# A conditioned feed-forward block in f32: out projection as seven quarter products, condition product on TensorE, means by adding DMAs, centring on GpSimd

## The reference, cut to what matters

```python
xr = x.reshape(Bx, Tx, 8, LATENT)                                # 8 groups of 128
h = jax.nn.gelu(jnp.einsum('btel,elf->btef', xr, W1) + b1, approximate=False)   # 128 -> 512
y = (jnp.einsum('btef,efl->btel', h, W2) + b2).reshape(Bx, Tx, Dx)              # 512 -> 128
eo = jax.nn.silu(emb) @ emb_W + emb_b                            # (4,1024) @ (1024,2048)
scale, shift = jnp.split(eo[:, None, :], 2, axis=-1)
hn = _layernorm(y, ln_g, ln_b) * (1.0 + scale) + shift
return x + jax.nn.silu(hn) @ out_W + out_b                       # 1024 -> 1024
```

## Time and profile before

| | |
|---|---|
| runs | 706.33, 706.30, 706.07 us; median 706.3 |
| span of the profiled execution | 704.2 us, 8302 instructions |
| busy | PE 700.5 us (99%), DVE 603.7 (86%), ACT 469.3 (67%), POOL 104.1 (15%) |
| granted PE clock, mean | 0.999 |
| DMA | 133.22 MB, mean 189 GB/s |

### The profile page before, as it was taken

How to read it: one execution, slowest core, us unless ns; L and a number is a source line. 1 busy time by engine, 2 the same in 40 slices (tenths; PEclk the granted TensorE clock), 3 DMA queues, 4 the chain that set the end, 5 groups by cost and what they waited for, 6 DMA issues and landing times.

```text
span 704.2 us, 8302 instructions
## 1 busy us (share of the span) xinstructions
PE 700.5 (99%) x3082; PEld 577.9 (82%) x3082; DVE 603.7 (86%) x725; ACT 469.3 (67%) x526; POOL 104.1 (15%) x68
## 2 busy tenths in 40 slices
PE   9999999999999999999999999999999999999998
PEld 6888888888888888888888888888888888888887
DVE  6888999999999989899887999999999978677512
ACT  7898888888878879888883456454656454555500
POOL 0000000000000011100121332423232432322100
PEclk9999999999999999999999999999999999999999
DMA  6766557344232531332789687887699877565531
GB/s 240 247 232 207 187 203 231 109 169 150 90 121 90 209 120 61 120 107 104 210 293 301 183 279 233 275 256 246 219 293 264 256 217 210 183 176 143 156 120 60
DMA packets 51880, 133.22 MB, mean 189 GB/s; under 512 B 4096, under 2 KB 25216, under 8 KB 49408
## 3 DMA queue, kind: packets, MB, share of 16 engines
q1 hardware_dynamic: 46944, 115.79, 46.9%
q0 software_dynamic: 4608, 16.78, 12.3%
q10 hardware_dynamic: 288, 0.13, 0.1%
HBM read 82.35 MB, written 33.55 MB: 165 GB/s over the span
## 4 chain that ended last, share of the span: by engine, by line
PE 99%; DMA 0%; ACT 0%; DVE 0%; issue 0%; DVEq 0%
PE psum L949 48%; PE psum L939 25%; PE psum L923 25%; PE psum L1001 2%; DMA wraw<-in_W 0%; PE psum L971 0%; ACT W L534 0%; DVE res L901 0%; DVEq L125 0%
## 5 line engine op out<-in xcount | busy, mean ns | idle before, releaser
L665 DVE TENSOR_TENSOR g_lo<-g_raw,g_hi 128x1024 fp32r<-128x1024 f32 x128 | 158.4, 1239 | 27.9 <-ACT g_hi L495 25.3
L489 ACT ACTIVATE g_raw<-psum,cols 128x1024 f32<-128x1024 f32 x128 | 142.9, 1116 | 34.1 <-PE psum L923 24.9
L949 PE MATMUL psum<-oW_hi,s_lo 128*128 128x512 f32 x496 | 152.7, 389 | 0.0
L949 PE MATMUL psum<-oW_hi,s_hi 128*128 128x512 f32 x496 | 152.7, 389 | 0.0
L949 PE MATMUL psum<-oW_lo,s_hi 128*128 128x512 f32 x496 | 152.6, 389 | 0.0
L939 PE MATMUL psum<-g_hi,W 128*128 128x512 f32 x512 | 136.8, 389 | 0.0
L923 PE MATMUL psum<-xT_hi,W 128*128 128x512 f32 x508 | 135.8, 389 | 0.0
L939 PEld LDWEIGHTS psum<-g_hi,W 128*128 128x128 f32 x512 | 96.1, 188 | 20.0
L923 PEld LDWEIGHTS psum<-xT_hi,W 128*128 128x128 f32 x508 | 95.3, 188 | 19.8
L949 PEld LDWEIGHTS psum<-oW_hi,s_hi 128*128 128x128 f32 x496 | 93.1, 188 | 19.4
L949 PEld LDWEIGHTS psum<-oW_hi,s_lo 128*128 128x128 f32 x496 | 93.1, 188 | 19.3
(11 more groups left out here) (77 smaller groups left out, 679.8 us busy)
## 6 DMA issues: line engine op xcount, KB each, us to landing
y_scratch<-y_stage SPq DMA_DIRECT2D x32, 512.0 KB, 3.1
yb<-y_scratch SPq DMA_DIRECT2D x16, 1024.0 KB, 4.8
res<-in_x SPq DMA_DIRECT2D x32, 512.0 KB, 6.1
res<-out_b_all POOLq DMA_DIRECT2D x32, 512.0 KB, 4.5
xT_raw<-in_xT SPq DMA_DIRECT2D x31, 512.0 KB, 4.3
out<-res SPq DMA_DIRECT2D x31, 512.0 KB, 4.1
tail_cols<-in_emb_T SPq DMA_DIRECT2D x24, 512.0 KB, 7.2
wraw<-in_out_W SPq DMA_DIRECT2D x16, 256.0 KB, 4.9
```

The lines of the kernel that those rows point to most:

```text
L489: nc.scalar.activation(g_raw[:, m % 2], ring(m), ACT.Gelu, bias=cols[:, R_B1 + k:R_B1 + k + 1]).then_inc(gelu_done, 1)
L665: nc.vector.tensor_tensor(g_lo[:, m % 2], g_raw[:, m % 2], g_hi[:, m % 2].bitcast(F32), ALU.subtract).then_inc(glo_done, 1)
L949: mm = nc.tensor.matmul(proj(q)[:, half], v[:, g, cut], w[:, g, half], start=(g == 0 and k == 0), stop=(g == G - 1 and k == 2))
```

## The change

The out projection of a pair is the product of a 2 x 2 block matrix A (token tiles 2p, 2p + 1 by feature halves 0 to 511, 512 to 1023) with out_W in quarters B11, B12, B21, B22. It is now computed in seven products of half-size blocks (the Strassen-Winograd form) instead of eight. DVE forms four sums of blocks of A (`sums12`, `sum3`, `sum4`), POOL four of out_W (T1 to T4, in stage 1). Each product is 12 matmuls of 512 columns (4 groups, 3 parts). The products P1, P2, P6, P5, P7, P3, P4 are made in this order; three go on accumulating into one PSUM bank `z`, two into `y5`, and DVE adds each bank to `res` after each product (`add`, seven times 512 columns per pair, instead of twice 1024). The weights of B22, T3 and T4 are written to DRAM in stage 1 (`wc_scratch`, split into hi and lo) and read back at the end of it, into places that stage 1 leaves.

The condition's product is 32 f32 matmuls on PE (`condition`), between chunks 24 and 25, from emb_W in SBUF (8 MB, loaded at items 1 to 4); DVE copies the result out, it goes through DRAM to be transposed (ACT's DMA at item 9), and there are no dots. The sums over groups for the mean are made by DMAs from POOL's queue that accumulate each `y_stage` tile into `y_sum` in DRAM (`add_y`); stage_y(n) waits until the one of n - 2 has landed. From pair 3 on POOL centres (`centre`, two of 128 x 1024 f32) and scales the mean, DVE does so for pairs 0 to 2. DVE's norm reads the reciprocal from PSUM, as before; one half of the squares goes to PSUM from pair 3 on.

```diff
...
+    y_sum = nc.dram_tensor("y_sum", [NP, P, TP], F32, kind="Internal").ap()
+    emb_rows = nc.dram_tensor("emb_rows", [B, NE * P], F32, kind="Internal").ap()
+    wc_scratch = nc.dram_tensor("wc_scratch", [3, 2, P, HG, BANK], F32, kind="Internal").ap()
...
+                    load_wc(C_T3, LO, t3)
+                    for q in range(2, 4):
+                        load_res(q)
...
             sp.wait_ge(glo_done, M)
+            load_wc(C_T3, HI, t3)
+            sp.wait_ge(s2_done, M)
+            load_wc(C_B22, HI, b22)
+            load_wc(C_B22, LO, b22)
+            load_wc(C_T4, LO, t4)
+            sp.wait_ge(y_staged, N)
+            g, t = ORDER[N - 1]
+            sp.dma_start(y_scratch[PT * t:PT * t + PT, :, g].rearrange("h p t -> p h t"),
+                         y_stage[:, (N - 1) % 2].rearrange("p (h t) -> p h t", h=PT)).then_inc(y_stored[(N - 1) % 2], 16)
+            sp.wait_ge(s_sum, 4)
+            sp.wait_ge(dlo_done, 1)
+            sp.wait_ge(alo_done, 1)
+            load_y(3)
             for s in range(2):
                 sp.wait_ge(y_stored[s], 16 * (N // 2))
+            for t in range(NT):
+                sp.wait_ge(y_summed[t], 16 * G)
+            load_wc(C_T4, HI, t4)
...
+            def add_y(n):
+                t = ORDER[n][1]
+                k = sums_before(n) - 1
+                pool.wait_ge(y_staged, n + 1)
+                place = y_sum[PT * t:PT * t + PT].rearrange("h p t -> p h t")
+                part = y_stage[:, n % 2].rearrange("p (h t) -> p h t", h=PT)
+                if k == 0:
+                    pool.dma_start(place, part).then_inc(y_summed[t], 16)
+                else:
+                    pool.wait_ge(y_summed[t], 16 * k)
+                    pool.dma_start(place, part, accum_op=ALU.add).then_inc(y_summed[t], 16)
...
+            def centre(p, h):
+                pool.wait_ge(y_landed[p % 3], 16 * (p // 3 + 1))
+                pool.wait_ge(mean_scaled, p - 2)
+                part = yb[p % 3][:, half_of(h)]
+                nc.gpsimd.tensor_tensor(part, part, mean_all[:].unsqueeze(1).to_broadcast([P, HG, TP]), ALU.subtract
+                                        ).then_inc(centred, 1)
+            def scale_mean(p):
+                pool.wait_ge(mean_done, p + 1)
+                nc.gpsimd.tensor_scalar(mean_all[:], mean_all[:], 1.0 / D, None, ALU.mult).then_inc(mean_scaled, 1)
+            for n in range(N):
+                ...
+                add_y(n)
             pool.wait_ge(out_b_landed, 16)
             for q in range(2):
                 add_bias(q)
+            for p in range(NP):
+                if p + 2 < NP:
+                    var_of(p + 2)
+                if 1 <= p and p + 3 < NP:
+                    mean_of(p + 3)
+                if p + 3 < NP:
+                    scale_mean(p + 3)
+                    centre(p + 3, 0)
+                    centre(p + 3, 1)
+                if p + 1 < NP:
+                    add_bias(2 * p + 2)
+                    add_bias(2 * p + 3)
...
+                if (n, c) == (VISIT + 3, 3):
+                    act.wait_ge(rows_stored, 4 * 16)
+                    act.dma_start(emb_dots[:], emb_rows.rearrange("b (q p) -> p b q", p=P), allow_slow_non_contiguous=True).then_inc(dots_landed, 16)
...
+            act.wait_ge(mod_step, 6)
+            silu(1, 0)
             stage_y(N - 1)
+            round_d(0, 2)
+            for p in range(NP):
                 if p + 1 < NP:
+                    silu(p + 1, 1)
+                    round_d0(p + 1)
+                    round_a22(p + 1)
+                if p + 2 < NP:
+                    nc.scalar.preload_act_table(ACT.Sqrt)
+                    root(p + 2, std_ps)
                     nc.scalar.preload_act_table(ACT.Silu)
+                if p + 1 < NP:
+                    round_d(p + 1, 1)
+                if p + 3 < NP:
+                    square(p + 3, 0)
+                    square(p + 3, 1)
+                if p + 2 < NP:
+                    silu(p + 2, 0)
+                if p + 1 < NP:
+                    round_d(p + 1, 2)
...
+            left, right = slice(0, BANK), slice(BANK, D)
+            for p in range(NP):
+                if p >= 1:
+                    add(p - 1, P4, z_ps(p - 1), 1, left)
+                rest_d(p, 2)
+                if p + 2 < NP:
+                    var_sum_first(p + 2)
+                add(p, P1, z_ps(p), 0, left)
+                if p + 2 < NP:
+                    var_sum_rest(p + 2)
+                if p + 1 < NP:
+                    rest_d0(p + 1)
+                add(p, P2, y2_ps, 0, left, of=P1)
+                if p + 1 < NP:
+                    sums12(p + 1)
+                    rest_a22(p + 1)
+                add(p, P6, z_ps(p), 0, right)
+                add(p, P5, y5_ps, 1, right)
+                if p + 2 < NP:
+                    invert(p + 2, rstd_ps, std_ps)
+                if p + 1 < NP:
+                    sum3(p + 1)
+                add(p, P7, z_ps(p), 1, right, of=P5)
+                if p + 2 < NP:
+                    norm(p + 2, 0, rstd_ps)
+                if p + 1 < NP:
+                    sum4(p + 1)
+                add(p, P3, y5_ps, 0, right, of=P6)
+                if p + 2 < NP:
+                    norm(p + 2, 1, rstd_ps)
+                if p + 1 < NP:
+                    rest_d(p + 1, 1)
...
+            def condition():
+                pe.wait_ge(cond_step, 2)
+                pe.wait_ge(emb_landed, 16 * KC)
+                pe.wait_ge(y_staged, VISIT)
+                for k in range(KC):
+                    for j in range(4):
+                        mm = nc.tensor.matmul(psum[32 * j:32 * j + B, VISIT_BANK], cond_s[:, k],
+                                              emb_raw[:, k, j * BANK:(j + 1) * BANK], start=(k == 0), stop=(k == KC - 1))
+                mm.then_inc(cond_done, 1)
+            def product(to, hi, lo, w_hi, w_lo, low_ready, begin=True, passes=range(3), cut=slice(0, BANK)):
+                for k in passes:
+                    v, w = ((hi, w_hi), (hi, w_lo), (lo, w_hi))[k]
+                    if k == 2:
+                        pe.wait_ge(*low_ready)
+                    for g in range(HG):
+                        mm = nc.tensor.matmul(to[:, cut], v[:, g], w[:, g, cut], start=(begin and k == 0 and g == 0),
+                                              stop=(k == 2 and g == HG - 1), skip_group_check=not begin)
+                if 2 in passes:
+                    mm.then_inc(prod_done, 1)
...
+                    begin_pair0(range(2))
+                if m == C * VISIT:
+                    condition()
...
+            for p in range(NP):
+                hi = [d_hi[(3 * p + i) % 4] for i in range(3)]
+                lo = [d_lo[(3 * p + i) % 4] for i in range(3)]
+                z = z_ps(p)
+                f, s = slice(0, HG), slice(HG, G)
+                if p == 0:
+                    begin_pair0(range(2, 3))
+                    pe.wait_ge(gelu_done, M)
+                else:
+                    if p >= 2:
+                        pe.wait_ge(added, 7 * (p - 2) + P4)
+                    pe.wait_ge(dhi_done, 3 * p + 1)
+                    product(z, hi[0][:, f], lo[0][:, f], wa[:, A_B11, HI], wa[:, A_B11, LO], (dlo_done, 3 * p + 1))
+                    pe.wait_ge(added, 7 * (p - 1) + P2)
+                product(y2_ps, hi[0][:, s], lo[0][:, s], wa[:, A_B21, HI], wa[:, A_B21, LO], (dlo_done, 3 * p + 1))
+                pe.wait_ge(dhi_done, 3 * p + 2)
+                pe.wait_ge(added, 7 * p + P1)
+                product(z, hi[1][:, f], lo[1][:, f], wa[:, A_T2, HI], wa[:, A_T2, LO], (dlo_done, 3 * p + 2), begin=False)
+                if p >= 1:
+                    pe.wait_ge(added, 7 * (p - 1) + P3)
+                product(y5_ps, hi[1][:, s], lo[1][:, s], wa[:, A_T1, HI], wa[:, A_T1, LO], (dlo_done, 3 * p + 2))
+                pe.wait_ge(dhi_done, 3 * p + 3)
+                pe.wait_ge(added, 7 * p + P6)
+                if p == 0:
+                    pe.wait_ge(wc_landed[C_T3], 32)
+                product(z, hi[2][:, f], lo[2][:, f], t3[HI], t3[LO], (dlo_done, 3 * p + 3), begin=False)
+                pe.wait_ge(added, 7 * p + P5)
+                if p == 0:
+                    pe.wait_ge(wc_landed[C_B22], 32)
+                product(y5_ps, hi[2][:, s], lo[2][:, s], b22[HI], b22[LO], (dlo_done, 3 * p + 3), begin=False)
+                pe.wait_ge(ahi_done, p + 1)
+                pe.wait_ge(added, 7 * p + P7)
+                if p == 0:
+                    pe.wait_ge(wc_landed[C_T4], 32)
+                if p < NP - 1:
+                    product(z, a_hi[p % 2], a_lo[p % 2], t4[HI], t4[LO], (alo_done, p + 1), begin=False)
+            for k in range(2):
+                product(last_ps[k], a_hi[p % 2], a_lo[p % 2], t4[HI], t4[LO], (alo_done, NP),
+                        cut=slice(k * TP, (k + 1) * TP))
```

(37 more changed lines are left out.)

871 lines of the change are left out of this document (415 added, 456 removed).

## The result

The changed kernel takes **838.1 us** (median of 4 runs, 836.2 to 840.0) against 706.3 (706.1 to 706.9): ratio 1.186, 95% interval 1.183 to 1.189. The forecast was 696, the range 678 to 717. It was wrong in sign, by 142 us.

A forecast was written before the change was run, and what follows sets the result against it. TensorE was taken to bound the kernel, 99% of the chain. 704.2 - 43.5 (seven products) + 8 (condition) + 0.5 (first stage) + 9.8 (VectorE against GpSimd) + 15 (change of stages) = 694.0; with 2.1, 696 us, range 678 to 717.

The forecast's parts named there:

- Seven products: Second stage, TensorE: a pair needs 84 matmuls instead of 96, 192 fewer over sixteen pairs; 43.5 us off.
- Condition: First stage, TensorE: 32 f32 products between two chunks, four sharing the array at once; 8 us on.
- Rival 1: Condition on TensorE: the f32 products don't overlap, 27.3 us instead of 8, total 715; chance 0.27.
- The loop through GpSimd: Second stage: one pair's round through GpSimd, ScalarE and VectorE takes 17.1 to 19.2 us with centrings of 2.3; just fits.
- VectorE against GpSimd: Second stage: overlap adds 0.9 us per reduction and 0.9 for both centrings; VectorE 19.7 a pair, 9.8 on over 14 pairs.
- Next to them stand mostly PSUM readers: Second stage: VectorE work beside GpSimd's centrings mostly reads PSUM, so both centrings together cost it only 0.9 us.
- Rival 2: Second stage: GpSimd holds VectorE through whole centrings, period 21.6 us, total 723; chance 0.13.
- First stage otherwise: First stage: VectorE and ScalarE stay ahead, GpSimd's y_sum transfers land in time; 0.5 us on, 0 to 10 allowed.
- Change of stages: Between stages: late second-stage weights, T4's high part last, stop TensorE in pair 0; 15 us on, range 5 to 20.
- The early bias wait lies inside the same wait: Change of stages: the late first bias, add P1 at 8 us or later instead of 4, adds nothing beyond the weight wait.
- The range: Whole kernel: forecast range 678 to 717 us, taking in rival 1 and half of rival 3, leaving out rival 2.

The follow-up runs named there:

- e9: e8 with the variance of pairs 3 to 15 as fp32r products on TensorE instead of VectorE's tree and GpSimd's reduction; 740.0 us, 739.9 when timed again.
- e1: The changed kernel with the second stage's centring back on VectorE, scaling folded in; GpSimd keeps reductions and bias transfers; 746.6 us.
- e4: The changed kernel with one GpSimd multiplication of 8 columns put between the two reductions, in 12 pairs; 995.8 us.
- e2: The changed kernel with a pair's two reductions as f32 products on TensorE, scaling gone, centring still on GpSimd; 762.4 us.
- e3: The changed kernel without the 32 adding transfers into y_sum and the waits on them, so its means are not the reference's; 810.4 us.
- e11: e1 with the adding transfers into y_sum made plain writes, so y_sum holds one group's y; 728.4 us.
- e10: e3 without GpSimd's 16 subtractions of out_W's quarters, so its output weights are not the reference's; 804.2 us.
- e5: e1 with the first two bias transfers issued ahead of the last adding transfer into y_sum; 755.0 us.
- e8: e1 with y_sum laid out in one 4 KB row per partition and item instead of shorter rows; 743.4 us.

## Why the prediction was wrong

- *Seven products, 43.5 off.* Right as a count of TensorE's work: matmuls are still 0.2267 us apart where nothing stops them, and e9's pairs come at 20.04 instead of 21.95. In the changed kernel none of it shows, as TensorE does not set the period.
- *Condition, 8 on.* Right: 7.05. Rival 1 is false.
- *The loop through GpSimd.* **This step failed, and is most of the 102 us of the second stage; with the centring taken off GpSimd (e1) 95 of them come back.** The loop had "two reductions 3.3 to 5.4, scaling 0.4, two centrings 2x, handovers 0.5". The centring was nearly right (2.4 to 3.4, mean 2.85, against 2.3 with 7.2 as the bound), the scaling was 0.9, and the part through ScalarE and VectorE, 8.3 by the rows, took 8.0 us or more. What had no term is GpSimd's change of code: 7.2 us from the reductions to the scaling, in full in each round, and 0.8 on average on the way back, where most of it hides beside the other engines' part. Together that is 8 of the 9 to 11 us between the forecast loop, 17.1 to 19.2, and the measured 27.8. The trace of before could not show it: there GpSimd ran no elementwise work in the second stage. I bounded the new operation's duration from both sides and never asked what stands between it and its neighbours. e4 puts the price at 6.6 us for each change added, and e1 and e2 take the changes away from either side.
- *VectorE against GpSimd, 0.9 for the two centrings.* Also wrong, and hidden behind the first error: 4.3 us a pair once the code no longer changes (e2). "Next to them stand mostly PSUM readers" failed; beside each centring an instruction with two SBUF inputs is caught and held until the centring has ended. Rival 2, with chance 0.13, named this, and put the period at 21.6; e2 has 21.92. That the two are near is luck: the 21.6 has 1.8 for reductions that e2 does not run, and 2.8 where e2 has 4.3. With the centring on VectorE the reductions cost about 1.1, less than the 1.8 I took, and the period is 20.38.
- *First stage otherwise, 0.5 on.* **Wrong: 37.6 on.** The step was "each transfer has two items, 21.8 us, before stage_y needs it, against 4.5 us to land for the accumulating ones now". The 4.5 is of an accumulation into SBUF, 4 KB rows; into DRAM it takes 8.8, and that still fits into two items: stage_y waits 0.2 us in all. What failed is that I priced only this wait. The transfers also keep x loads from landing (5.5 us instead of 4.3), and ScalarE, which takes x, gelu, out_W and y in one order, stands on a landing in front of 17 of its roundings of x. By the runs: sums in y_sum 18 (e3), of which the adding is 13 at this place (e11); GpSimd's subtractions 7.6 (e10, not clear of the spread); 12 remain, which I did not take apart. Candidates are the out_W roundings on ScalarE and VectorE, and loads of out_W that land in 12 us.
- *Change of stages, 15 on, T4's high part last.* The size was near (20.6), the place wrong: T4 is never waited for in the changed kernel, the first bias is. "The early bias wait lies inside the same wait" was the wrong way round. The sum of bytes over the rate gave the end of the stretch well: the DMA engines are full until 424, e5's reordering only moves the gap, and the 28.6 us of the forecast's sum, or 25, counted from the end of the first stage's matmuls near 399.5 end at 428 or 424. But it says nothing of when a single transfer lands in such a stretch: at 2.7 us each the last add_y and the first two biases would have been early, and they took 15.5 and 18.9. It also lacked the restart at the lower clock: the eight matmuls after the gap take 3.75 us instead of 1.98.
- *The range.* Each term had its own bounds, and none had room for a cost of a kind that no row shows. The first stage alone (37) is beyond the 10 that I left it.

## What to carry to other kernels

Before you give an idle engine a second kind of work, ask what it pays to change kinds, and put that price into each loop that passes through it: here 13.1 us of GpSimd's work came round only every 28. An engine at 32% is not free capacity for VectorE's work either, since a VectorE operation with two SBUF inputs stood still beside it, 4.3 us a pair in e2. And a transfer that is "hidden" still takes DMA time from the loads that are not: price the engines' share, not only its own deadline.

## What was not expected of the hardware

- GpSimd's change of code between a partition reduction and an elementwise operation: 5.8 to 7.7 us in e4 around an operation of 8 columns, and up to 11.3 in front of the scaling, every time.
- An adding transfer of 0.5 MB from SBUF into DRAM lands in 8.8 us (median of 32) and the same without adding in 6.1; in e8 the number of rows hardly mattered (8.2 with a quarter as many rows per byte).
- A centring of 128 x 1024 on GpSimd takes 2.4 to 3.4 us against VectorE's 1.21, and VectorE's 0.68 us operations with two SBUF inputs take 2.8 beside it.
